# Delta rule, last inverse level: the two 64-row products of a pair of chunks issued by turns, head by head

## The reference, cut to what matters

```python
def step(state, inp):
    q_t, k_t, v_t, a_t, b_t = inp
    retained = jnp.einsum('bhvk,bhk->bhv', state, k_t)
    rk = retained[..., None] * k_t[:, :, None, :]
    vk = v_t[..., None] * k_t[:, :, None, :]
    state = a4 * (state - b4 * rk) + b4 * vk
    o_t = jnp.einsum('bhvk,bhk->bhv', state, q_t)
    return (state, o_t)
```

## Time and profile before

| | |
|---|---|
| median of three runs | 3808.57 us |
| the profiled execution | 3808.81 us |
| its span, first to last instruction | 3806.2 us |
| PE busy | 3262.9 us (86%) |
| VectorE busy | 2396.6 us (63%) |
| ScalarE busy | 1356.5 us (36%) |
| L1485, 512 records, busy | 113.4 us, mean 419 ns |
| the delta stage | about 1690 to 3190 us of the span |

### The profile page before, as it was taken

One profiled execution on the slowest core, in us unless ns is written; L12 is line 12 of the kernel. 1 busy time (PEld: TensorE's weight loads), 2 busy tenths in 40 slices (PEclk: granted clock), 3 DMA queues, 4 the chain that ended last, 5 costly groups with the idle time before them and its releaser, 6 DMA issues. The chain is left out here.

```text
span 3806.2 us, 52445 instructions
## 1 busy us (share of the span) xinstructions
PE 3262.9 (86%) x18666; PEld 2525.1 (66%) x18666; DVE 2396.6 (63%) x5801; ACT 1356.5 (36%) x2713; POOL 158.4 (4%) x158
## 2 busy tenths in 40 slices
PE   5999938888999999747989898989898989488887
PEld 2665524445999999714867686868686869355554
DVE  6788425554777777766685858576767673354542
ACT  2333202221444444314534444444444442033232
POOL 0000000015111111000000000000000000000000
PEclk8999958999999999968797988888888886588786
DMA  1000080022899989741011111110111100100000
GB/s 62 23 17 12 11 160 12 11 75 81 305 322 317 320 318 323 253 152 64 34 34 35 34 36 34 35 34 35 34 35 34 35 20 1 53 12 23 12 17 12
DMA packets 203686, 327.31 MB, mean 86 GB/s; under 512 B 37449, under 2 KB 157522, under 8 KB 202258
## 3 DMA queue, kind: packets, MB, share of 16 engines
q1 hardware_dynamic: 196930, 305.94, 24.4%
q0 software_dynamic: 6480, 17.77, 1.2%
HBM read 275.15 MB, written 48.50 MB: 85 GB/s over the span
## 5 line engine op out<-in xcount | busy, mean ns | idle before, releaser
L767 PE MATMUL ex_ps<-ex_xbT,ex_w 128*128 128x128 f32 x4544 | 531.2, 275 | 1.7 <-DMA ex_b<-in_b_all_dram 1.2
L767 PEld LDWEIGHTS ex_ps<-ex_xbT,ex_w 128*128 128x128 f32 x4544 | 524.3, 192 | 6.1 <-DMA ex_b<-in_b_all_dram 1.8
L1378 PE MATMUL de_ps<-de_hT,de_w 128*128 128x512 f32 x640 | 306.2, 636 | 27.6 <-DMA de_w<-in_w_kqv_dram 13.9
L896 ACT ACTIVATE ex_t<-ex_ps,ex_b 128x128 f32<-128x128 f32 x568 | 208.8, 368 | 337.0 <-PE ex_ps L767 319.1
L1378 PEld LDWEIGHTS de_ps<-de_hT,de_w 128*128 128x128 f32 x640 | 129.0, 207 | 188.1 <-issue 186.0
L711 PE MATMUL ex_ps<-ex_xT,ex_w 128*128 128x512 f32 x512 | 230.6, 607 | 12.5 <-DVE ex_gl L1008 9.1
L1008 DVE SCALAR_TENSOR_TENSOR ex_gl<-ex_ps,ex_b,ex_t 128x128 f32<-128x128 f32 (+1 forms) x316 | 123.7, 391 | 137.3 <-ACT ex_t L896 69.4
L711 PEld LDWEIGHTS ex_ps<-ex_xT,ex_w 128*128 128x128 f32 x512 | 98.0, 195 | 131.8 <-issue 115.0
L1735 DVE SCALAR_TENSOR_TENSOR de_ya<-de_kx,de_taps,de_ya 128x512 f32<-128x512 f32 x192 | 142.5, 751 | 49.2 <-ACT de_ya L1574 44.7
L1008 DVE SCALAR_TENSOR_TENSOR ex_gm<-ex_ps,ex_b,ex_t 128x128 f32<-128x128 f32 (+1 forms) x316 | 121.8, 385 | 48.9 <-ACT ex_t L869 46.6
L177 PE MATMUL mx_ps<-mx_hT,mx_w_in 128*128 128x512 f32 x320 | 143.6, 605 | 8.3 <-ACT mx_hT L249 8.3
(11 more groups left out here) (378 smaller groups left out, 6268.3 us busy)
## 6 DMA issues: line engine op xcount, KB each, us to landing
ex_w<-in_w_all_dram SPq DMA_DIRECT2D x144, 1024.0 KB, 6.5
ex_w<-in_w_all_dram SPq DMA_DIRECT2D x72, 512.0 KB, 8.6
de_w<-in_w_kqv_dram SPq DMA_DIRECT2D x80, 256.0 KB, 2.8
de_ab<-alpha_d SPq DMA_DIRECT2D x8, 2048.0 KB, 8.3
ex_xb<-ex_xs_d SPq DMA_DIRECT2D x71, 129.0 KB
ex_xs_d<-ex_blank SPq DMA_DIRECT2D x71, 128.5 KB, 8.3
ex_w<-ex_y_d SPq DMA_DIRECT2D x16, 512.0 KB, 6.1
mx_xin<-in_x_dram SPq DMA_DIRECT2D x8, 512.0 KB, 4.0
```

The lines of the kernel that those rows point to most:

```text
L767: m = pe.matmul(ps[:, n % 4, x * BLK:(x + 1) * BLK], w[:, k, part * HID + c * P:part * HID + (c + 1) * P], xbT[sx][:, k, :], start=(k == 0 ...
L896: act.activation(t1[:, n % 2, 0:BLK], ps[:, n % 4, 0:BLK], ACT.Identity, bias=b13[s][:, 0, n:n + 1]).then_inc(t1_ready, 1)
L1378: m = pe.matmul(ps[:, n % 2, :], w[:, g % SLOTS, k, n % 2 * P:(n % 2 + 1) * P], hT[:, k, :], start=(k == 0), stop=(k == KT - 1))
```

## The change

On PE the first product of c0 stays a run of 8 heads. Then PE waits for `x11` of c1 and for `y6` of c0, and issues the first product of c1 and the second product of c0 by turns, one head of each. Then it waits for `y6` of c1 and issues the second product of c1 as a run. Nothing is changed on the other engines, and the number of matmuls, their operands and their banks are the same.

```diff
-                    for c in both:
-                        pe.wait_ge(s["x11"], b * NC + c + 1)
-                        for hd in range(H):
-                            m = pe.matmul(ps[:, 2 + c % 2, hd * HALF:(hd + 1) * HALF], DG[0:HALF, c, hd, :], X11[0:HALF, c % 2, hd, :],
-                                          start=True, stop=True, skip_group_check=True)
-                        m.then_inc(s["y6p"], 1)
-                    for c in both:
-                        pe.wait_ge(s["zeroed"], 1)
-                        pe.wait_ge(s["y6"], b * NC + c + 1)
-                        for hd in range(H):
-                            m = pe.matmul(ps[0:HALF, 4 + c % 2, hd * HALF:(hd + 1) * HALF], Y6[HALF:P, c % 2, hd, :], XT[HALF:P, c, hd, HALF:P],
-                                          start=True, stop=True, skip_group_check=True)
-                        m.then_inc(s["x6p"], 1)
+                    c0, c1 = both
+
+                    def lower_times_upper(c, hd):
+                        return pe.matmul(ps[:, 2 + c % 2, hd * HALF:(hd + 1) * HALF], DG[0:HALF, c, hd, :], X11[0:HALF, c % 2, hd, :],
+                                         start=True, stop=True, skip_group_check=True)
+
+                    def times_lower(c, hd):
+                        return pe.matmul(ps[0:HALF, 4 + c % 2, hd * HALF:(hd + 1) * HALF], Y6[HALF:P, c % 2, hd, :], XT[HALF:P, c, hd, HALF:P],
+                                         start=True, stop=True, skip_group_check=True)
+
+                    pe.wait_ge(s["x11"], b * NC + c0 + 1)
+                    for hd in range(H):
+                        m = lower_times_upper(c0, hd)
+                    m.then_inc(s["y6p"], 1)
+                    pe.wait_ge(s["zeroed"], 1)
+                    pe.wait_ge(s["x11"], b * NC + c1 + 1)
+                    pe.wait_ge(s["zeroed"], 1)
+                    pe.wait_ge(s["y6"], b * NC + c0 + 1)
+                    for hd in range(H):
+                        m = lower_times_upper(c1, hd)
+                        if hd == H - 1:
+                            m.then_inc(s["y6p"], 1)
+                        m = times_lower(c0, hd)
+                    m.then_inc(s["x6p"], 1)
+                    pe.wait_ge(s["zeroed"], 1)
+                    pe.wait_ge(s["y6"], b * NC + c1 + 1)
+                    for hd in range(H):
+                        m = times_lower(c1, hd)
+                    m.then_inc(s["x6p"], 1)
```

## The result

| | before | after |
|---|---|---|
| median of 4 runs each (us) | 3809.18 (3808.51 to 3810.11) | 3833.51 (3829.94 to 3836.10) |
| ratio to before | 1 | 1.0063, 95% interval 1.0046 to 1.0080 |
| profiled execution, its span (us) | 3808.81, 3806.2 | 3835.59, 3833.8 |

The change makes the kernel slower by 24 us. The forecast was 3877 us, slower by 68: the sign is right, the size is not. The time lies inside the range, 4.5 us above its lower end. The new lines are L1485 (first product), L1489 (second product) and L1516 (the product with the scaled keys, L1500 before); L1509, L1518 and L1523 have become L1525, L1534 and L1539, and DVE's L1880 is L1896.

What follows compares the result with a forecast made beforehand. TensorE (PE) was taken to set the pace in the delta stage. Stalls and shape changes add 4.29 us a pair, x 16 = +68.6 us, on 3808.6 us: 3877 us, +1.8%, range 3829 to 3905.

Steps and rivals of the forecast that it cites:

- What bounds the kernel: In the delta stage PE sets the pace, 168.8 us busy per 187.73 us batch; work added to its queue moves the end.
- Step 1: First product of c0, a run of 16 records, stays as it was: 3.25 us from first to last start.
- Step 2: PE waits for y6 of c0 before the first product of c1: 1.20 us instead of 0.213, +0.99 a pair.
- Step 3: Turns of the two products pay for shape changes: 1.013 us per head, 8.10 against 5.12 us, +2.98 a pair.
- Steps 4 and 5: Second stall for y6 of c1, +0.58 us; last run of the second product, boundary already counted, -0.19 us a pair.
- The cover: After the pair, DVE's and ACT's work for later PE products stays hidden, at no cost.
- The clock: The place of the clock's rise in L1500 may move, -13 to +14 us in all; taken as 0.
- A: Rows 0 to 63 and 64 to 127 work at once, hiding the second product; 3811 us, not slower; chance 0.09.
- B: Order stays serial, but short visits to the other shape cost nothing, only stalls remain; +21 us, 3829; chance 0.05.
- C: Halves overlap and denser work brings the clock to 1.00 in the pair; 99 us less, 3710; chance 0.03.
- D: The change doesn't act as issued, but at least the first stall stays; +16 us, 3825; chance 0.03.

Runs made afterwards that it cites:

- e1: Changed kernel with its waits kept, but both products in whole runs of 8 heads instead of turns; 3776.46 us, ratio 0.9919.
- e4: Kernel before, in its grouped order, with the first product on only the 64 weight columns that are read; 3748.30 us, ratio 0.9852.
- e2: Changed kernel with turns of two heads of each product instead of one, same waits; 3855.14 us, ratio 1.0136.
- e3: Changed kernel with turns, the first product on only the 64 weight columns read, so both products have one shape; 3716.92 us, ratio 0.9762.
- e5: Kernel before with eight extra dense matmuls (512 moving columns, results unread) ahead of the last scan; 3780.68 us, ratio 0.9938.
- e10: e4 with four extra dense matmuls (512 moving columns, results unread) ahead of the last scan; 3720.42 us, ratio 0.9780.
- e6: Changed kernel with 32 extra thin matmuls (one moving column, results unread) ahead of the last scan; 3867.47 us, ratio 1.0168.
- e7: Kernel before with the one-column products by `ones` ahead of the query products in each batch's tail; 3762.91 us in two groups, ratio 0.9887.
- e8: e4 with the products by `ones` put ahead of the query products, as in e7; 3751.74 us, ratio 0.9863.
- e9: e3 with the products by `ones` put ahead of the query products, as in e7; 3814.17 us over ten runs, ratio 1.0022.
- e11: e3 with the same four extra dense matmuls ahead of the last scan as e10; 3721.89 us, ratio 0.9779.

## Why the prediction was right in place and wrong in size

**What bounds the kernel.** Right. What was added on PE's queue moved the end, in e1 to e4 too, once the clock is taken out.

**Step 1, the first run.** Right: from 2787.84 to the end of sixteen records, 3.67 us by the timeline.

**Step 2, the new stall.** Right but for 0.10 us. PE starts again at 2792.39. DVE's operation, after:

```profile
2791.55 0.69 DVE L1896 TENSOR_TENSOR de_PQ<-de_ps,de_scT 64x512 f32<-64x512 f32 x1 [1.18 <-PE de_ps L1485]
```

It ends at 2792.24, so PE resumes 0.15 us after it where I took 0.05 from a release by ACT. The second gap ends 0.15 us after its DVE operation as well; twice 0.10, less a few hundredths in the turns and the last run, are the whole 0.14 by which the pair is off. e1 has the same gap of 0.88.

**Step 3, the turns.** Right to the hundredth: 1.01 us per head (2793.99 - 2792.98), with L1485 to L1489 in 0.59 to 0.61 us (forecast 0.27 + 0.35) and back in 0.40 (0.16 + 0.24). The price taken from the two boundaries of the old order held for all sixteen new ones. e2 confirms it by halving their number. e3 shows the cause, with the reserve on the columns said there: with one shape there is no such price, and the halves overlap. The Trainium skill (TensorEngine Tiling (Array Packing), Key Properties) states both halves of this, that a change of mode drains and a change of tile does not, and the runs agree, with 0.39 us for a round trip at 1.2 GHz.

**Steps 4 and 5.** The second gap is 0.48 us of idle time, within the 0.3 to 0.6 named, and the last run of L1489 is as forecast.

**The cover.** DVE's and ACT's work behind it stayed hidden, as forecast; no new wait of PE on them appears from L1516 to the end of the batch. That batch is 194.56 us long, 6.8 more than 187.73, against the 8.6 forecast (2 x 4.29): 8.9 in the two pairs, less some 2 by the clock behind them.

**The clock: here the prediction failed.** Its words were "I take 0", with bounds that looked only at L1500, the product right behind the edit. For all that PE does from there to the next batch, and for the last scan, it put the clock's effect at nothing without giving a reason; this is the step that failed. Within those bounds the piece itself came out right: -7.6 us over the sixteen, inside -13 to +14. But the clock was followed no further. The batch period shows one more part of it: after the tail of a batch the next batch's first projections come at a lower clock before than after. Before, and then after:

```profile
2814.71 16.70 PE L1378 MATMUL de_ps<-de_hT,de_w 128*128 128x512 f32 x32 [2.26 <-issue]
```

```profile
2859.53 13.99 PE L1378 MATMUL de_ps<-de_hT,de_w 128*128 128x512 f32 x32 [1.76 <-issue]
```

2.7 us less in this batch, by a clock of 0.84 (window 2814.71:2831.41) that becomes 1.00 (2859.53:2873.52); the third piece of the table as a whole is 8.0 us less over seven batches, so other parts of it lost some. And the last batch, which I never looked at, gave 32.0. In sum 70.8 - 7.6 - 8.0 - 32.0 = 23.2, and the medians differ by 24.3. The same sum with the forecast's terms: 68.6 in the pairs and 0 for the other three.

How much of this is shown: that the clock of the last scan is worth about 30 us of the total is shown by e5 and e10 (put to 1.00 from outside: -24 and -28 us, the added work of 7 and 3.5 included) and by e6 (put back to 0.50: +34 us over the median of after, +38 with each taken against the kernel before of its own series, of which 10 are the added work). Whether it is the kind of the added work or the mere delay before the scan that sets the level, these runs do not separate: no thin work was added where the scan was at 0.50. The 7.6 and the 8.0 us are read from the two traces alone. What it is in the pairs of after, of e1 and of e3 that leaves the last scan at 1.00, and in those of e2 and e4 at 0.50, is open. What PE does directly ahead of the scan is the same in all of them, sixteen products by `ones`, and neither the length nor the idle time of the pair sorts them: after 15.0, e1 11.7 and e3 7.7 us on one side, e2 13.3, before 10.6 and e4 6.7 on the other. One thing in the traces does sort them: the product with the scaled keys, where the clock rises after each pair, takes 81 to 83 us in sum in after, e1 and e3, and 89 to 94 in before, e2, e4, e7 and e8. Where the rise came sooner, the last scan stayed at 1.00. e9 is an exception (82.4 us and a scan at 0.50), with another order between the two. That is an observation on eight kernels and no mechanism; e7 counts in it by its one trace, a run of its long group, though its other group seems to have had the scan at 1.00, and no run set the place of the rise by itself.

Could it have been foreseen? The level after could not, but that it mattered could: the window 3188.9 to 3252.0 of the trace of before, 63 us of busy PE at a clock of 0.50, was there to be read. At twice the clock it is about 31 us shorter, so the forecast had two values, 3877 and some 3846, and its own range should have begun 31 us lower, at 3819. From 3846 to the measured 3833.5 it is mostly the 7.6 and the 8.0 us.

**The rivals.** A (the halves work at once) is false for this change, by the serial steps of 0.6 and 0.4 us, and true as soon as both have one shape (e3). The condition that I set against it, "those all have one shape", was the right one, as far as e3 tells (its reserve on the columns stands there). The Trainium skill (TensorE: Matmul & The Clock Gate, Part 3, The mechanism) has the rule without this condition; e3 agrees with it, the change does not. B (a short visit costs nothing) is refuted by the same steps, although the measured time lies 4.5 us from its 3829: a total near a rival's number was no evidence for its mechanism. C is refuted by the clock of 0.50 in the pair, though its other half, that the clock gives back time, came true far away from the pair. D is refuted by the timeline.

## What to carry to other kernels

Two products on different rows of the array ran at once here where their shapes were the same, and never where they differed, so make the shapes equal first, by leaving out the columns that nobody reads. That alone took 3.9 us off a pair (e4); turns on top of it overlapped the products but made the pair longer again, by their waits (e3); and turns between the two shapes cost 0.39 us each round at 1.2 GHz. Look in every trace for long stretches in which PE is never idle and yet at 0.50: the one here went on or off with edits elsewhere and was worth 30 us, where the edited pairs cost 71, so such a stretch belongs into the range. Judge an edit by its own stretch and the total by all its pieces; e1 has 18 us more in its pairs than before and is 29 us faster, and e2 has less in them than after and is slower.

## What the runs showed of the hardware that was not expected

- A stretch of the same code on PE, without idle time, ran at 1.2 GHz for 63 us (before, from its second microsecond on) or at 2.4 GHz for all of 34 us (after) and did not change level on the way. With 3.5 to 7 us of products with 512 moving columns ahead of it, it ran at the high level (e5, e10; e11, where it did so without them too, in e3); with 10 us of products with one, at the low one (e6).
- One kernel, e7, had runs of two lengths 35 us apart on one chip in one series, with mean granted clocks of 0.88 and 0.87.
- In e9 the alternation of 128 and one moving columns stayed at 0.50 in all batches; in e3 the same lines in the other order ran at 1.00; in e7 and e8 the order of e9 ran at 0.88 on the mean.
- With equal shapes the overlap needs no turns at a border: in e4 the first record of the second product (2712.07) stands ahead of the last one of the first product, since the timeline lists 31 records of L1486 before it, not 32, and the last one starts at 2712.09.
- Turns with overlap gained less than nothing on the spot: 7.68 us a pair on the mean in e3 against 6.74 in e4, since the two waits cost more than the 1.8 us that the overlap saves.
